# Two adapter layers on one core: a's low part, layer 0's addition, the experts' choice and the x turns of tile 1 in another order

## What is computed

```python
# layer 0: one adapter for each batch entry
Bx  = einsum('bni,bri->bnr', x, B[adapter_ids])
x   = x + einsum('bnr,bor->bno', Bx, A[adapter_ids])
# layer 1
base   = einsum('btd,od->bto', x, W)
logits = einsum('btd,ed->bte', x, Wr) + one_hot(language_ids) * 5.0
topw, topi = top_k(logits, 2)
gates  = sum(one_hot(topi) * softmax(topw))
h      = einsum('btd,erd->bter', x, A1)
x      = x + base + 2.0 * einsum('bter,bte,eor->bto', h, gates, B1)
```

## Time and profile before

| | before |
|---|---|
| median of 3 runs | 535.11 us (534.6 to 536.44) |
| profiled execution, whole | 534.09 us |
| its span | 532.3 us |
| mean granted clock of TensorE | 0.994 of full speed |
| PE busy | 521.4 us, 98% |
| DVE busy | 326.7 us, 61% |
| ACT busy | 210.6 us, 40% |
| POOL busy | 173.1 us, 33% |

### The profile page before, as it was taken

The page is one execution under the profiler, slowest core; times in us unless marked ns, Lnnn a source line. Parts: engine busy times, 40 slices in busy tenths (PEclk is TensorE's granted clock), DMA queues, the critical chain, the costliest instruction groups (busy, mean ns, idle before and its releaser), DMA issues.

```text
span 532.3 us, 9378 instructions
## 1 busy us (share of the span) xinstructions
PE 521.4 (98%) x3500; PEld 478.2 (90%) x3500; DVE 326.7 (61%) x829; ACT 210.6 (40%) x493; POOL 173.1 (33%) x162
## 2 busy tenths in 40 slices
PE   5999999999999999999999999999999999999997
PEld 5888899998999999899998989999898999989897
DVE  4888676655567665556765555685555667555321
ACT  3646433425344242525424353443435334343211
POOL 6462222434331343422234342223433223341100
PEclk9899999999999999999999999999999999999999
DMA  8933523444332444433244433324443333421101
GB/s 330 321 102 98 154 89 89 129 129 129 89 116 77 107 128 129 115 99 107 68 129 129 129 109 97 104 79 129 128 123 99 101 102 94 129 89 41 41 40 41
DMA packets 30865, 60.42 MB, mean 114 GB/s; under 512 B 4316, under 2 KB 20060, under 8 KB 30820
## 3 DMA queue, kind: packets, MB, share of 16 engines
q1 hardware_dynamic: 24144, 38.81, 24.0%
q0 software_dynamic: 6656, 20.98, 13.5%
q10 hardware_dynamic: 20, 0.03, 0.0%
HBM read 43.02 MB, written 16.78 MB: 112 GB/s over the span
## 4 chain that ended last, share of the span: by engine, by line
PE 88%; DVE 7%; ACT 2%; issue 1%; POOL 1%; DMA 0%; ACTq 0%; DVEq 0%
PE o_bank L469 70%; PE o_bank L482 8%; PE x_bank L388 4%; PE b_bank L370 3%; DVE a_raw L746 1%; DVE x_bank L728 1%; PE b_bank L358 1%; DVE w_lo L703 1%; DVE x_lo L703 1%; ACT bx_pair L617 1%; DMA ids<-in_itok_B_dram 0%; PE o_bank L458 0%; PE o_bank L358 0%; DVE top_no L806 0%; POOL a_in L274 0%
## 5 line engine op out<-in xcount | busy, mean ns | idle before, releaser
L469 PE MATMUL o_bank<-w_hi,x_hi 128*128 128x512 f32 (+1 forms) x744 | 257.0, 345 | 0.0
L469 PE MATMUL o_bank<-w_lo,x_hi 128*128 128x512 f32 (+1 forms) x744 | 251.4, 338 | 0.0
L469 PE MATMUL o_bank<-w_hi,x_lo 128*128 128x512 f32 (+1 forms) x744 | 251.3, 338 | 0.0
L299 POOL TENSOR_TENSOR a_t<-a_raw,a_t 64x1024 fp32r<-64x1024 f32 x30 | 72.1, 2402 | 282.7 <-ACT a_t L590 282.7
L469 PEld LDWEIGHTS o_bank<-w_hi,x_hi 128*128 128x128 f32 x744 | 141.0, 189 | 12.2 <-issue 3.0
L469 PEld LDWEIGHTS o_bank<-w_hi,x_lo 128*128 128x128 f32 x744 | 139.8, 188 | 10.2
L469 PEld LDWEIGHTS o_bank<-w_lo,x_hi 128*128 128x128 f32 x744 | 140.2, 188 | 8.9
L599 ACT COPY xt<-x_bank 128x512 f32<-128x512 f32 x64 | 37.6, 587 | 122.6 <-DVE x_bank L728 119.6
L728 DVE STREAM_TRANSPOSE x_bank<-x_in 128x512 f32<-128x512 f32 x60 | 68.4, 1186 | 0.0
L274 POOL DMA_INDIRECT a_in<-in_L_cond_A_dram,a_run x64 | 60.9, 951 | 19.2 <-issue 19.1
L746 DVE STREAM_TRANSPOSE a_raw<-a_in 128x1024 f32<-128x1024 f32 x32 | 63.5, 1985 | 0.0
(11 more groups left out here) (102 smaller groups left out, 486.0 us busy)
## 6 DMA issues: line engine op xcount, KB each, us to landing
out_dram<-out_sb SPq DMA_DIRECT2D x31, 512.0 KB, 2.9
x_in<-in_x_dram SPq DMA_DIRECT2D x120, 128.0 KB, 3.5
w_in<-in_L_cond_W_dram SPq DMA_DIRECT2D x6, 512.0 KB, 8.7
x_in<-in_x_dram SPq DMA_DIRECT2D x2, 512.0 KB, 3.3
out_sb<-in_L_cond_W_dram SPq DMA_DIRECT2D x2, 512.0 KB, 15.1
a_in<-in_L_cond_A_dram,a_run POOLq DMA_INDIRECT x64, 3.4
w_in<-in_L_cond_A_dram SPq DMA_DIRECT2D x1, 512.0 KB, 4.4
b_in<-in_L_cond_B_dram,b_run POOLq DMA_INDIRECT x32, 2.9
```

Of the source, the lines that this page charges most:

```text
L299: nc.gpsimd.tensor_tensor(lower, a_raw[Q:P, :], lower.bitcast(F32), ALU.subtract).then_inc(a_lo_ready, 1)
L469: mm = pe.matmul(O[part][:, 0:hi - lo], xs[:, n % 2, c, :], w[:, c, lo:hi], start=(k == 0), stop=(k == K3 - 1), skip_group_check=True)
```

## The change

Four edits, all for tile 1 (n = 1) or for a of tile 2.

1. a's low part of tile 2 is made by POOL, between `reload(3)` and `reload(4)`, no longer by DVE.
2. On PE layer 0's addition for tile 2 stands behind part 1, no longer between parts 0 and 1. In the other tiles it stays.
3. On ACT exp comes before xt(3).
4. On DVE the choice comes first; the x turns of tile 3 and gt_hi and gt_lo follow it, ahead of x_lo of tile 2.

```diff
@@ gpsimd @@
             load_b(2)
             reload(3)
+            a_lo_part(2, 3, 3)
             reload(4)
@@ tensor @@
-                if n + 1 < T:
+                if 1 < n < T - 1:
                     add_l0(n + 1)
                 make_part(n, 1, 0, 18)
                 turn_gated(n)
                 make_part(n, 1, 18, K3)
+                if n == 1:
+                    add_l0(2)
                 make_part(n, 2, 0, 12)
@@ scalar @@
                 if n == 1:
                     a_hi_part(2)
+                exp_part(n)
+                if n == 1:
                     xt_part(3)
-                exp_part(n)
@@ vector @@
-                if n == 1:
-                    a_lo_part(2)
-                    xT_part(3)
                 choose_experts(n)
                 weigh_experts(n)
+                if n == 1:
+                    xT_part(3)
+                    gated_t_part(n)
                 if n + 1 < T:
                     x1_lo_part(n + 1)
-                gated_t_part(n)
+                if n > 1:
+                    gated_t_part(n)
```

## The result

The changed kernel took **536.36 us** (median of 22 runs, 535.63 to 537.39), the kernel before 535.43 in the same number (533.87 to 536.44): a ratio of 1.002, 95% interval 1.0012 to 1.0027. The forecast was 535.8, in a range of 534.6 to 537.1, as 0.7 us slower; measured are 0.9 us by the medians and 1.1 by the ratio, two tenths of a per cent.

What follows compares the result with a forecast made beforehand. PE, busy 98%, was taken as the bound, with a DVE and ACT chain setting tile 2's turn. Waits removed, 1.2 us, against about 1.9 added: net +0.65, rounded to 0.7; 535.11 + 0.7 = 535.8 us, range 534.6 to 537.1.

Steps and rivals of the forecast that it cites:

- PE's lead behind tile 1: PE from tile 1's part 2 on: 1.2 us ahead, from a turn 2.1 earlier less 0.9 for the addition.
- DVE's second gap: Tile 1, between gt_lo and x_lo(2): 0.6 us idle for ACT's x_hi(2); x turns of tile 4 0.65 us later.
- The shift of the turn: Tile 2, PE's turn of gated(2): 0.65 us later, down the chain over DVE and ACT, at about 71.3.
- POOL beside DVE: Tile 1, POOL's low part beside DVE's choice: cost between 0 and 0.4 us, taken as under 0.1.
- rival C: Tile 1, lock at full length: the whole choice waits for POOL; 0.9 to 1.1 us more, 536.7 to 536.9; chance 0.07.
- B: Rival, tile 2: gain only absorbed, ACT's x_hi(2) doesn't hold DVE up, gated's turn stays at 70.63; 535.1 us; chance 0.07.
- D: Rival, tile 2: PE's waits drop the clock to 1.2 GHz for 6.5 us; 3.2 us more, 539.0; chance 0.05.
- E: Rival, tile 2: chain to gated(2) doesn't hold PE, which keeps 1.2 us and wins 0.2 too; 533.7 us; chance 0.04.

Runs made afterwards that it cites:

- the kernel with the low part on POOL alone: The kernel before with one edit of the four, a's low part of tile 2 on POOL; ratio 0.9993 (0.9984 to 1.0002) to the kernel before.
- the two repeats: The kernel before and the changed kernel profiled once more, nothing edited; bx_t(2) to the turn of gated(2) 22.99 and 23.79 us.
- the spare turn: Changed kernel plus an unneeded DVE turn of 0.67 us directly ahead of tile 4's x turns; ratio 1.0024 to the kernel before.

## Why the forecast held

**Tile 1.** logit(1) was expected 1.3 us of idle after bx_t(2), and it was 1.32. The turn of gated(1) was expected at 51.8 to 52.0, 4.2 to 4.4 from bx_t(2), without a wait over 0.2; it came at 4.11. PE's lead behind tile 1 was expected as 1.2 us and was 1.42 (part 2 starts 5.97 from bx_t(2), 7.39 before); at make_bx(3) it gave back 0.52 of that (60.60 - 48.99 against 60.14 - 47.63), where 0.3 was expected. So 0.9 was left, as expected, but by two misses that cancel.

**DVE's second gap.** Expected 0.6, measured 0.69. That it comes from xt(3) ahead of x_hi on ACT was argued from the rows, and the kernel with these two exchanged shows it: 0.68 us of distance for that gap. One step was put at nothing without a reason. I let the x turns of tile 4 start at x_lo's end, and they start 0.11 behind it; in the kernel before they stood behind gt_lo and started at 55.56, 0.08 before its end:

```profile
55.35 0.29 DVE L703 TENSOR_TENSOR gt_lo<-b_bank,gt_hi 128x128 fp32r<-128x128 f32 x1
```

So the x turns of tile 4 were 0.81 late and not 0.65, and it is by the shorter turns of b and a, which I had not foreseen, that PE's turn is late by 0.74 only.

**Tile 2.** The waits were expected as 0.4 before the addition and 1.3 at the turn of gated(2); they are 0.28 and 1.18. Their sum with b's 0.41 is 1.87 (expected about 1.9). The shift of the turn was expected as 0.65, rounded up to 0.7, and is 0.74.

**POOL beside DVE.** I had taken under 0.1 for it, and the choice shows 0.15. In tile 1 top_no takes 0.30 where it takes 0.17 in tile 2, and ends at 51.64 while POOL's piece ends at 51.61:

```profile
49.13 2.48 POOL L299 TENSOR_TENSOR a_t<-a_raw,a_t 64x1024 fp32r<-64x1024 f32 x1 [11.16 <-ACT a_t L593]
...
51.34 0.30 DVE L810 CAST top_no<-top_at 128x2 f32<-128x2 uint32 x1
...
71.14 0.17 DVE L810 CAST top_no<-top_at 128x2 f32<-128x2 uint32 x1
```

In each of the nine profiles where POOL's piece ends while top_no runs, top_no takes 0.28 to 0.33 and ends 0.02 to 0.03 behind it. In the kernel with the low part on POOL alone it starts at 50.80, behind POOL's end at 50.40, and takes 0.17. From logit to the end of gated it was 2.35 us, against the 2.20 that I had taken: of the 0.15, 0.13 is top_no. That the chain isn't 0.15 later for it is luck of the estimate: the x turns of tile 3 start 0.08 before gated's end and took 2.21 instead of 2.29, so they end 6.15 from bx_t(2), where I had 6.17. logit and the two searches of the maximum took 0.16, 0.17 and 0.16, as ever, though POOL worked beside them, and so did the two x turns in the kernel with the low part on POOL alone (2.17, 2.29 before). So rival C, which had the whole choice wait, is out. (One reading was wrong without an effect: a_hi(2) had ended at 47.69, and what DVE's start at 48.02 followed was its own bx_t(2), which ended at 47.98.) By the Trainium skill, page "SBUF — State Buffer", section "SBUF: two separate sides", the loser of the shared port pair blocks until the other is through, and on DVE it is an operation in a 2-port mode or with two SBUF inputs that asks for the pair. The end of top_no agrees with the first; in which mode it ran no run here shows.

**The rivals.** B (absorbed, no loss) would have needed DVE's second gap away, and is what the exchange on ACT made. D, the clock: it stayed at 1.00 around tile 2's waits, so they cost only their own length. It did so from 50 us on in all twelve profiles. The comparison with the start, on which D rested, was less firm than it looked: a wait of 1.57 us that ended at 10 us was followed by a fall to 0.50 in one profile of the changed kernel, and by none in the other. The stretches from 67 to 73 and from 73 to 80 us, busy time by engine, then PEclk, DMA share and GB/s:

```profile
67.00:73.00 6.00, 4.54 (x31) 3.85 (x30) 4.20 (x21) 2.44 (x7) 2.79 (x3) 1.00 0.35 109
73.00:80.00 7.00, 7.00 (x46) 6.78 (x45) 5.97 (x8) 2.88 (x6) 0.00 (x0) 1.00 0.01 2
```

E (the gain stays) is refuted from both sides: the addition put back costs PE 1.3 to 2.2 us in tile 1 and 0.2 in the end, and time is won only where the chain over DVE and ACT is made shorter.

**What was mis-sized.** By the distance the loss is 0.74, by the runs 0.9 to 1.1; the interval of the ratio (0.6 to 1.4 us) takes in both. What lies between them stays open: behind the turn of gated(2) the executions are alike, so it would lie ahead of bx_t(2), where no edit acts; the two repeats can't settle it, since the start spreads by more than that. And the rule by which I priced an added DVE instruction, its whole duration, is too high in a chain of semaphore waits (0.34 for 0.67).

## What to carry to other kernels

The longest wait of the bounding engine need not be the one that is worth removing: ask at its next wait which chain ends there, and follow that chain back past the edit. Here a chain over DVE and ACT ended in tile 2's turn with 0.20 us of wait on PE, so 1.4 us won on PE in tile 1 were worth nothing, and of 0.8 us lost on DVE 0.7 counted. When work is taken out of an in-order queue ahead of an instruction that waits for another engine, the queue gets a gap and not a lead; what pays is to put work of the chain into the gap.

Where executions differ in their start by more than the effect, measure from the last untouched instruction to the first one behind the change. Two profiles of each of two kernels agreed in that to 0.05 us, where their spans differed by 1.1 and 1.6.

## What had not been expected of the hardware

A DVE instruction that waits for no semaphore, put between two that do, costs less than it lasts: 0.67 us moved the next start by 0.42 and cost 0.34. Of the first difference, 0.25, 0.19 is that the spare turn starts 0.08 before x_lo's end and takes away the step of 0.11 behind it. The start of an execution, up to bx_t(2), spreads over 2.8 us between profiles of kernels that are the same up to there, and by 0.6 to 1.1 us within each of three sets from one chip. A cast of 128x2 that ran into a POOL subtraction ended with it, 0.02 to 0.03 behind, in nine profiles of nine.
